# A factorization-machine layer on one core: the eighth quad of every block but the last is scaled and added like the others, where it was summed raw by TensorE

## The reference

```python
gathered = jax.vmap(lambda table, idx: table[idx], in_axes=(0, 1), out_axes=1)(emb, xi)
e = gathered * xv[:, :, None]
s = jnp.sum(e, axis=1)
qi = 0.5 * (s * s - jnp.sum(e * e, axis=1))
h = jax.nn.relu(xv @ W1 + b1)
x = jnp.concatenate([qi, h], axis=1)
return x @ W2 + b2
```

## Time and profile before

| What | Value |
|---|---|
| Median of 3 runs | 735.56 us |
| The profiled execution's own time | 734.71 us |
| Its span | 732.9 us |
| DVE busy | 540.5 us (74%) |
| POOL busy | 485.9 us (66%) |
| ACT busy | 474.2 us (65%) |
| PE busy | 123.1 us (17%) |
| Bytes gathered | 130.06 MB, 180 GB/s over the span with the rest |

### The profile page before, as it was taken

One profiled execution on the slowest core, in us unless ns is written; L12 is line 12 of the kernel. 1 busy time (PEld: TensorE's weight loads), 2 busy tenths in 40 slices (PEclk: granted clock), 3 DMA queues, 4 the chain that ended last, 5 costly groups with the idle time before them and its releaser, 6 DMA issues.

```text
span 732.9 us, 2598 instructions
## 1 busy us (share of the span) xinstructions
PE 123.1 (17%) x374; PEld 29.6 (4%) x374; DVE 540.5 (74%) x463; ACT 474.2 (65%) x516; POOL 485.9 (66%) x524
## 2 busy tenths in 40 slices
PE   2030020300303003030211302203030220400315
PEld 0000000000000000000000000001000000000001
DVE  4675969595398683988969396396978849549684
ACT  0877775771875837778683863868777394567871
POOL 6777775762767737777774754777777474677760
PEclk9995555555555555555555555555555555555557
DMA  7777775772766737777774763777777474577760
GB/s 226 203 204 203 204 203 158 203 204 56 202 192 185 205 102 204 203 204 204 203 202 128 202 179 98 203 203 204 203 204 202 126 203 132 145 203 203 203 190 0
DMA packets 33683, 131.93 MB, mean 180 GB/s; under 512 B 8641, under 2 KB 8769, under 8 KB 33634
## 3 DMA queue, kind: packets, MB, share of 16 engines
q0 software_dynamic: 32768, 130.06, 64.6%
q1 hardware_dynamic: 800, 1.31, 0.6%
q10 hardware_dynamic: 98, 0.40, 0.2%
HBM read 131.72 MB, written 0.01 MB: 180 GB/s over the span
## 4 chain that ended last, share of the span: by engine, by line
POOL 39%; issue 23%; another core or an unknown queue 6%; PE 3%; DVE 2%; ACT 1%; DMA 0%; POOLq 0%
POOL gathered L218 39%; DVE running_ps L462 1%; PE sum_ps L328 1%; PE hidden_ps L349 1%; ACT squares L241 1%; ACT squares L247 1%; PE hidden_ps L362 1%; PE sum_ps L341 1%; DMA gathered<-emb,index_rows 0%; DVE squares L435 0%; DVE gathered L447 0%; POOLq L214 0%; DVE weighted_late L547 0%; DVE weighted L421 0%
## 5 line engine op out<-in xcount | busy, mean ns | idle before, releaser
L218 POOL DMA_INDIRECT gathered<-emb,index_rows x512 | 484.4, 946 | 224.1 <-issue 155.8
L462 DVE SCALAR_TENSOR_TENSOR running_ps<-gathered,running_ps 128x1984 f32<-128x1984 f32 x77 | 171.4, 2226 | 146.7 <-issue 107.6
L435 DVE SCALAR_TENSOR_TENSOR squares<-squares,w_ps 128x1984 f32<-128x1984 f32 (+1 forms) x128 | 276.7, 2167 | 0.0
L234 ACT ACTIVATE gathered<-gathered,values 128x496 f32<-128x496 f32 x312 | 194.5, 695 | 25.5 <-DMA gathered<-emb,index_rows 23.3
L241 ACT ACTIVATE squares<-gathered 128x5952 f32<-128x5952 f32 x31 | 159.8, 5156 | 36.8 <-DMA gathered<-emb,index_rows 34.3
L341 PE MATMUL sum_ps<-added_up,own_sample 128*32 128x496 f32 x128 | 30.1, 1031 | 550.3 <-issue 431.0
L247 ACT ACTIVATE squares<-gathered,values 128x496 f32<-128x496 f32 x76 | 47.4, 696 | 67.4 <-DMA gathered<-emb,index_rows 63.2
L362 PE MATMUL hidden_ps<-w_b,value_rows 33*128 33x512 f32 x64 | 55.3, 1011 | 42.4 <-issue 20.8
L234 ACT ACTIVATE running_ps<-gathered,values 128x496 f32<-128x496 f32 x64 | 39.5, 662 | 33.7 <-issue 18.7
L254 ACT ACTIVATE sum_squared<-sum_ps 128x496 f32<-128x496 f32 x16 | 9.2, 573 | 71.0 <-remote 58.4
L462 DVE SCALAR_TENSOR_TENSOR added_up<-gathered,running_ps 128x1984 f32<-128x1984 f32 x16 | 35.5, 2219 | 25.4 <-ACT gathered L234 25.0
(11 more groups left out here) (40 smaller groups left out, 27.0 us busy)
## 6 DMA issues: line engine op xcount, KB each, us to landing
gathered<-emb,index_rows POOLq DMA_INDIRECT x512
w_all<-w SPq DMA_DIRECT2D x1, 760.0 KB
values<-value SPq DMA_DIRECT2D x1, 256.0 KB, 2.9
value_rows<-value_t ACTq DMA_DIRECT2D x1, 256.0 KB
index_raw<-index SPq DMA_DIRECT2D x1, 240.0 KB, 4.3
w_b<-w ACTq DMA_DIRECT2D x1, 128.0 KB
index_raw<-index SPq DMA_DIRECT2D x1, 16.0 KB, 2.5
w_b<-b ACTq DMA_DIRECT2D x1, 4.0 KB
```

What stands on the lines that cost most here:

```text
L218: nc.gpsimd.indirect_dma_start(out=gathered[:, n % slots, j, :], out_offset=None, in_=emb, in_offset=bass.IndirectOffsetOnAxis(ap=index_ro ...
L234: return nc.scalar.mul(running_ps[:, j, 0:dim] if s == 0 else rows_of_one, rows_of_one, values[:, g:g + 1])
L435: return nc.vector.scalar_tensor_tensor(of, of, -0.5, w2_ps[:, 0:dim].unsqueeze(1).to_broadcast([P, quads_of.stop - quads_of.start, dim]), ...
L462: nc.vector.scalar_tensor_tensor(added_up[:, i % 2] if last_add(n) else sums, gathered[:, n % slots], 1.0, sums, ALU.mult, ALU.add).then_i ...
```

## The change

The raw quad is kept in the last block alone. In the other blocks ScalarE scales quad 7 as well, VectorE adds seven quads, and the add that writes to `added_up` is that of quad 7. Quad 4 is still the one that VectorE scales. TensorE's matmuls on the raw quad and the table `weights` with the four instructions that filled it go. `summed` is raised by the last of the four `own_sample` matmuls. POOL waits on `added` and `squared` for every quad. ScalarE squares quads 4 and 5 together behind the scaling of quad 7, and quads 6 and 7 together once quad 0 of the next block has landed. VectorE reads the hidden layer at quad 6 instead of 7, and weighs the squared sums at quad 7 instead of 6.

```diff
-    block_quads = (7,)
-    wide = [0, 1, 2, 3, 4, 5, 6]
-    by_vector = 4
+    wide = [0, 1, 2, 3, 4, 5, 6, 7]
+    by_vector = (4,)
     adds = len(wide) - 1
     def by_tensor(n):
-        return n % quads in (end_quads if n // quads == end else block_quads)
+        return n // quads == end and n % quads in end_quads
...
     def last_add(n):
-        return n % quads == (3 if n // quads == end else 6)
-    square_of = {0: 1, 1: 2, 2: 2, 3: 2, 7: 3, 4: 4, 5: 4, 6: 4}
+        return n % quads == (3 if n // quads == end else 7)
+    square_of = {0: 1, 1: 2, 2: 2, 3: 2, 4: 3, 5: 3, 6: 4, 7: 4}
...
                         pool.wait_ge(squared, squared_with(n - slots))
-                        if by_tensor(n - slots):
-                            pool.wait_ge(summed, (n - slots) // quads + 1)
-                        else:
-                            pool.wait_ge(added, adds_with(n - slots))
+                        pool.wait_ge(added, adds_with(n - slots))
...
                 elif s == 7:
-                    square_scaled(n - 3, 3)
+                    place_free(n)
+                    square_scaled(n - 3, 2)
+                elif s == 0 and i > 0:
+                    square_scaled(n - 2, 2)
...
-                pe.wait_ge(added, adds_with(i * quads + (3 if i == end else 6)))
-                sum_fields(i)
+                pe.wait_ge(added, adds_with(i * quads + (3 if i == end else 7)))
+                last = sum_fields(i)
                 if i < end:
-                    sum_quad(i * quads + 7).then_inc(summed, 1)
+                    last.then_inc(summed, 1)
...
-            for j in range(GROUPS):
-                spread(weights[:, :, j], values[:].rearrange("p (i s j) -> p i s j", s=quads, j=GROUPS
-                                                             )[:, :, quads - 1, j], blocks, j)
...
-                if s == 6 and i > 0:
+                if s == 7 and i > 0:
                     weigh_sums(i - 1)
-                if s == 7 or n == end * quads + 4:
+                if s == 6 or n == end * quads + 4:
                     dve.wait_ge(hidden_ready, i + 1)
```

More of the change, by code:

```diff
@@ L39, in fm_kernel, with scaled_wide_with @@
     end_quads = (4, 5, 6, 7)
-    block_quads = (7,)
-    wide = [0, 1, 2, 3, 4, 5, 6]
-    by_vector = 4
+    wide = [0, 1, 2, 3, 4, 5, 6, 7]
+    by_vector = (4,)
     adds = len(wide) - 1
     def by_tensor(n):
-        return n % quads in (end_quads if n // quads == end else block_quads)
+        return n // quads == end and n % quads in end_quads
+    by_scalar = [s for s in wide[1:] if s not in by_vector]
     def scaled_with(n):
-        return n // quads * (adds - 1) + adds_with(n % quads) - (n % quads > by_vector)
+        i, s = divmod(n, quads)
+        return i * len(by_scalar) + max(sum(k <= s for k in by_scalar), 1)
+    def scaled_wide_with(n):
+        i, s = divmod(n, quads)
+        return i * len(by_vector) + sum(k <= s for k in by_vector)
     def adds_with(n):
@@ L95, in fm_kernel @@
         own_group = sb("own_group", [P, GROUPS])
-        weights = sb("weights", [P, blocks, GROUPS, COLS])
         end_weights = sb("end_weights", [P, deep, GROUPS, COLS])
@@ L105, in fm_kernel @@
         added_up = sb("added_up", [P, 2, GROUPS, dim])
-        weights_sum = sb("weights_sum", [P, GROUPS + 1])
+        weights_sum = sb("weights_sum", [P, 1])
         weighted = sb("weighted", [P, dim])
@@ L263, in square_scaled @@
                 act.wait_ge(scaled, scaled_with(n + count - 1))
-                if n % quads == by_vector:
-                    act.wait_ge(scaled_wide, n // quads + 1)
+                if any(n % quads <= s < n % quads + count for s in by_vector):
+                    act.wait_ge(scaled_wide, scaled_wide_with(n + count - 1))
                 square(n, count, slice(0, GROUPS)).then_inc(squared, 1)
@@ L300, in _ @@
                 if by_tensor(n):
-                    if s == (deep if i == end else quads - 1):
+                    if s == deep:
                         place_free(n)
                     square_quad(n)
-                elif s > 0 and s != by_vector:
+                elif s in by_scalar:
                     if s == 1:
@@ L325, in sum_rows @@
             def sum_rows(n, j):
-                i, s = n // quads, n % quads
-                operand = end_weights[:, s - deep, j] if i == end else weights[:, i, j]
-                return nc.tensor.matmul(sum_ps[j * COLS:(j + 1) * COLS, 0:dim], operand,
+                s = n % quads
+                return nc.tensor.matmul(sum_ps[j * COLS:(j + 1) * COLS, 0:dim], end_weights[:, s - deep, j],
                                         gathered[:, n % slots, j], start=False,
@@ L341, in sum_fields @@
                     last = nc.tensor.matmul(sum_ps[j * COLS:(j + 1) * COLS, 0:dim], own_sample[:],
-                                            added_up[:, i % 2, j, :], start=True, stop=False,
+                                            added_up[:, i % 2, j, :], start=True, stop=(i < end),
                                             tile_position=(0, j * COLS))
+                return last
             def late_squares(n):
@@ L356, in _ @@
             pe.wait_ge(own_sample_ready, 1)
-            pe.wait_ge(weights_ready, GROUPS + 1)
+            pe.wait_ge(weights_ready, 1)
             for i in range(blocks):
@@ L444, in add_quad @@
                     dve.wait_ge(squared, squared_with(n - 1))
-                elif s == by_vector:
+                elif s in by_vector:
                     dve.wait_ge(fetched[n % slots], (n // slots + 1) * 16 * GROUPS)
@@ L450, in add_quad @@
                         ALU.mult, ALU.mult).then_inc(scaled_wide, 1)
-                    dve.wait_ge(scaled_wide, i + 1)
+                    dve.wait_ge(scaled_wide, scaled_wide_with(n))
                 else:
@@ L484, in _ @@
                 running_ps[:, :, dim:dim + blocks],
-                values[:].rearrange("p (i s j) -> p s j i", s=quads, j=GROUPS)[:, by_vector]
+                values[:].rearrange("p (i s j) -> p s j i", s=quads, j=GROUPS)[:, by_vector[0]]
             ).then_inc(values_kept, 1)
@@ L492, in spread @@
                     accum_out=weights_sum[:, unread:unread + 1]).then_inc(weights_ready, 1)
-            for j in range(GROUPS):
-                spread(weights[:, :, j], values[:].rearrange("p (i s j) -> p i s j", s=quads, j=GROUPS
-                                                             )[:, :, quads - 1, j], blocks, j)
             spread(end_weights[:].rearrange("p s j c -> p (s j) c"), values[:, gathers - deep * GROUPS:],
-                   deep * GROUPS, GROUPS)
+                   deep * GROUPS, 0)
             dve.wait_ge(w1_loaded, 48)
```

## The result

The change made the kernel slower: 742.31 us (742.15 to 743.29, 4 runs) against 735.15 us of the kernel before on the same chip, ratio 1.0106 with an interval of 1.0079 to 1.0134. The forecast was 669 us.

What follows compares the result with a forecast made beforehand. The prediction took the bound to be TensorE's debt, growing with its matmuls and stalling the gathers. From the profiled 734.71 us it took 66.8 us, other costs 0, giving 667.9, plus 0.85 to the median: 669 us, range 664 to 703.

Steps and rivals of the forecast that it cites:

- the 66.8 us of stalls: POOL's eight long waits before quad 7 gathers, beyond the usual 0.30 us each, read as waits for TensorE's `summed`.
- The price of 2.80 us for a matmul record: TensorE's signals: the hidden layer's 11.21 us over 4 records, taken as the cost of each matmul record.
- the growth of 12 to 16 us a block: TensorE: 20 records need 51.8 us against 40.0 us of gathers, so it falls behind by this much each block.
- POOL no longer waits on `summed`: POOL before quad 7: dropping this wait gains 66.8 us if nothing else takes its place.
- TensorE's debt no longer grows: TensorE without the raw quad's 8 records: 12 remain, 30.5 to 33.6 us a block, under 40.0.
- The costs taken as 0: VectorE's extra add, ScalarE's scaling and squaring, `place_free`, the `weights` instructions and the end: each counted as hidden, 0 us.
- The forecast of the loop: VectorE's last add ends at 543.2, ScalarE's next sum begins at 545.09: 1.9 us of room, cost 0.
- ScalarE's squaring: One squaring of three quads becomes two of two: +1.8 us, ScalarE at 31.6 us of 40, cost 0.
- A: Rival: TensorE's debt shrinks but does not vanish; at 42 us a block 701 us; chance 0.15.
- C: Rival: the loop of VectorE and ScalarE takes over, each block growing by 1.5 us; 693 us; chance 0.09.
- B: Rival: TensorE's lateness unrelated to its matmuls; stalls return at ScalarE's wait on `summed`; about 735 us; chance 0.05.
- D: Rival: slower, `summed` late in every block within the loop through ScalarE's scaling; up to 857 us; chance 0.09.

Runs made afterwards that it cites:

- b_no_raw_sums_3: Kernel before without TensorE's matmuls on the raw quad, `summed` raised by the last matmul on `added_up`; chip C, late signals: 736.59 us, 0.9981.
- after_third: The changed kernel, unaltered, run again on chip A, where signals are prompt: 661.89 us, 1.0002 of the kernel before.
- b_no_raw_sums_2: Kernel before without TensorE's matmuls on the raw quad, on chip A, where signals are prompt: 661.62 us, 1.0000.
- a_squares_together: Changed kernel with quads 4 to 7 squared by one ScalarE instruction instead of two; chip D: 734.01 us, 0.9998 of the kernel before.
- a_pool_count: `a_squares_together` plus four tiny GpSimd memsets a block; chip E: 732.73 us, 0.9991 of the kernel before.
- a_one_scale_3: Changed kernel with ScalarE scaling each quad in one instruction by a constant instead of four; chip D: 731.39 us, 0.9964 of the kernel before.
- a_two_by_vector_2: Changed kernel with quad 6 scaled by VectorE too; chip D: 731.14 us, 0.9960 of the kernel before.
- a_plus_small_3: Changed kernel plus two short ScalarE instructions (128x1, unread) a block; chip C: 751.13 us, 1.0173 of the kernel before.
- a_vector_count: `a_squares_together` plus seven tiny VectorE memsets a block, one before each add; chip E: 745.05 us, 1.0170 of the kernel before.

## Why the prediction was wrong

*The reading of the bound* was right for the kernel before: the 66.8 us of stalls were released by late signals of TensorE, and its lateness did grow with its matmuls. The price of 2.80 us for a matmul record is two records of 1.40, the matmul and its weight load (11.21 us is 8 x 1.40), and the growth of 12 to 16 us a block was measured as 16.

*What failed* is the step from there to the gain: "POOL no longer waits on `summed`. Gain 66.8 us if nothing else takes its place", with ScalarE's added work at cost 0. It took TensorE for the only engine with a debt, because "no engine is near full", which is true of busy time alone. Something else did take its place: on such a chip ScalarE's 33 instructions need 46.2 us a block and GpSimd's 32 need 44.8, where the forecast had 40.0. `b_no_raw_sums_3`, with 24 records of TensorE a block instead of 40 and all else as before, is 0.2% faster, not 9%. I never asked whether the other engines' instructions cost the same 1.40 us; their counts stand in the earlier trace rows.

*"TensorE's debt no longer grows"*: right. Line 255 had no wait in any block but the last, and the recorded signals of TensorE are at most 3.1 us late (24 x 1.40 = 33.6 us, under 40.0).

*"POOL no longer waits on `summed`, gain 66.8 us"*: the waits went and 58.7 us came back on `squared`, at 46.2 us a block instead of 44.7. Of the forecast gain 4.2 us were left at the last gather, and the end took 12.5 us.

*The costs taken as 0* were right as far as busy time and order go, and `after_third`, without late signals, shows them in isolation: 661.89 against 661.77 us of the kernel before, for some 30 us more of VectorE and 26 us more of ScalarE (569.3 and 500.2 us busy; 539.7 and 474.0 in `b_no_raw_sums_2`, which has the old programs of both). The forecast of the loop (1.9 us of room) held: 0.8 us of waiting for the landing is left in each block.

*ScalarE's squaring* was costed at +1.8 us of busy time and hidden. On a chip with late signals its price is not its time but its being one instruction more: three quads in one became four in two, 32 became 33. `a_squares_together` gives that one back, and with it the 1.1%.

*The rivals.* A and C had their own signs and neither came. B said that the stalls would come back and gave 735 us; in time it is the nearest, but by luck: its premise, that TensorE's lateness has nothing to do with its matmuls, is refuted by the trace of the kernel before, and it put the stalls at ScalarE's wait on `summed`, where they came at ScalarE's own `scaled`. D had the sign and neither the place nor the size. That a program whose gathers stand still for 67 us for no visible reason may do so because of the chip was not among the rivals; that was a large omission, since it makes the forecast gain not just wrong but, on a prompt chip, impossible.

By the Trainium skill, "TensorE: Matmul & The Clock Gate", section "The cost: per-tile semaphore tail", each increment that a matmul of TensorE makes on completion costs some 26 ns. On chip A the traces agree in size (0.03 to 0.06 us from the last matmul's end to `summed`); with late signals they show 42.8 us in the kernel before.

## What to carry to other kernels

When signals come late and every engine is half idle, count each engine's instructions in a steady period, TensorE's weight loads and VectorE's reads of its accumulator included, and multiply by the pace (here 1.40 us). Every engine whose product is above the period that you hope for can be expected to bind (`a_pool_count` is the exception here), not only the one whose late signals the profile shows now: relieving that one gave nothing here, because two more stood at 44.8 us or above. A mean that fits is not enough; the engine's own late signals, or its instructions stretched to the pace, must be there too. Then fewer and larger instructions on the fullest engine pay (`a_squares_together`). And run the kernel before on a second chip before explaining a stall: here 66.8 us of it were not there. All of this was measured in recorded runs; whether an unrecorded program keeps such a pace is not shown.

## What the hardware showed that was not expected

- **Two kinds of chip.** The kernel before took 661 us on chip A and 733 to 738 us on B to E and in the first result; the changed kernel's busy times on A and in the first result are the same.
- **A pace of 1.400 us per instruction**, on ScalarE, VectorE, GpSimd and TensorE each, whatever the instruction does: on VectorE a memset of 0.06 us counts like an add of 2.2 us, though it raises no semaphore. GpSimd's memsets are the exception: they counted in two blocks only.
- **It begins late.** The first blocks run at full speed, up to five of them. Counting 1.40 us for each instruction issued and taking off the time that has passed (never below nothing), GpSimd was some 37 us ahead when its gathers began to be stretched, at 224 us in `a_one_scale_3` and, having been slower until then, at 310 us in `a_two_by_vector_2`; in `a_pool_count` it was 45 us ahead at 131 us. ScalarE stood at 24 to 28 us at its stalls in the changed kernel, `a_squares_together` and `b_no_raw_sums_3`. In the kernel before ScalarE never gets beyond 22 us and GpSimd beyond 26, which fits that neither is held there. So an engine has room for some 17 to 32 instructions, then the pace binds. That what it has run ahead is owed at the end, as the changed kernel's 17.8 us suggest, is a reading and was not tested.
- **Late signals are also absent ones**: on chips B to E and in the first result most semaphore updates are missing from the records, on chip A hardly any. Between 50 and 700 us the changed kernel's first trace has 66 to 72 updates in each 50 us, one per 0.70 us, which is half of 1.40; on chip A it has some 670. In the kernel before, the three stretches in which TensorE's lateness falls to nothing have 182 to 196.
- *Open*: what keeps the pace. The regular spacing of the recorded updates points at the recording itself, as a rival to a slower chip: every run here, the timed ones too, comes with its span and clock, so no run shows what an unrecorded launch takes. Open too: why GpSimd's memsets stopped counting after two blocks, why TensorE's lateness falls to nothing after 37 to 42 us, and whether the pauses of `a_plus_small_3` and `a_vector_count` are the same thing.
